# A gated cross-attention block on one core: SyncE's turn in another order, context for two pairs at once, and the sums read back from the scratch in one transfer

## The reference, cut to what matters

```
v, k = ctx @ Wv + bv, ctx @ Wk + bk          # per batch, 16 heads of 16
q    = layernorm(x) @ Wq + bq
energy = q . k, masked; attn = softmax(energy / 4)
x = x + tanh(g_xattn) * ((attn @ v) @ Wo + bo)
h = layernorm(x) @ W @ W1 @ W2
x = x + tanh(g_ffn) * tanh(h + bias)
```

## Time and profile before

| what | value |
|---|---|
| time, median of 3 runs (lowest, highest) | 1143.55 us (1141.15, 1146.37) |
| the profiled execution, its own time | 1153.29 us |
| its span in the profile | 1151.5 us |
| busy: PE / DVE / ACT / POOL | 90% / 81% / 72% / 70% |
| DMA engines, mean busy share in the steady part | 52% to 54% |
| granted TensorE clock, mean | 0.978 of full |

### The profile page before, as it was taken

The page is one execution under the profiler, slowest core; times in us unless marked ns, Lnnn a source line. Parts: engine busy times, 40 slices in busy tenths (PEclk is TensorE's granted clock), DMA queues, the critical chain, the costliest instruction groups (busy, mean ns, idle before and its releaser), DMA issues.

```text
span 1151.5 us, 45278 instructions
## 1 busy us (share of the span) xinstructions
PE 1041.1 (90%) x18487; PEld 905.1 (79%) x18487; DVE 937.6 (81%) x1331; ACT 834.5 (72%) x1275; POOL 801.2 (70%) x1184
## 2 busy tenths in 40 slices
PE   5989989999999999999999989989999999999964
PEld 4767878887888888888778778878788788888854
DVE  4778788788888888888888788788887787888766
ACT  4466778677787777777787777777776786777742
POOL 5256677677777777777777777677776676777753
PEclk9899999999999999999999999999998999999998
DMA  5134455555555555555555455555545454554432
GB/s 154 41 95 128 130 141 152 139 142 153 145 155 139 154 152 145 148 154 155 139 154 143 140 150 144 144 145 144 161 133 138 139 144 137 140 159 122 115 114 90
DMA packets 260400, 158.87 MB, mean 138 GB/s; under 512 B 174945, under 2 KB 227170, under 8 KB 260194
## 3 DMA queue, kind: packets, MB, share of 16 engines
q1 hardware_dynamic: 260050, 155.72, 48.5%
q10 hardware_dynamic: 144, 0.26, 0.1%
HBM read 85.92 MB, written 68.94 MB: 134 GB/s over the span
## 4 chain that ended last, share of the span: by engine, by line
PE 34%; DMA 26%; SPq 23%; issue 11%; DVE 5%; POOL 1%; ACT 0%; DVEq 0%; POOLq 0%
DMA scratch_y<-yn 12%; PE ps_m L502 8%; PE ps_s L623 6%; SPq L299 6%; PE ps_s L602 6%; DMA q_aug<-scratch_m 5%; SPq L288 4%; DMA scratch_m<-max_T 4%; PE ps_m L564 4%; PE ps_m L495 4%; SPq L271 3%; PE ps_x L634 2%; PE ps_s L608 2%; SPq L258 2%; SPq L281 2%
## 5 line engine op out<-in xcount | busy, mean ns | idle before, releaser
L1006 DVE TENSOR_TENSOR probs<-ps_s,far_T 128x2048 f32<-128x2048 f32 x128 | 293.3, 2291 | 99.5 <-PE ps_s L623 93.2
L995 DVE TENSOR_REDUCE neg_max<-ps_s 128x16 f32<-128x2048 f32 x128 | 292.6, 2286 | 60.0 <-PE ps_s L608 59.8
L797 ACT ACTIVATE probs<-probs 128x2048 f32<-128x2048 f32 x128 | 244.6, 1911 | 6.7 <-DVE probs L1006 6.6
L623 PE MATMUL ps_s<-q_aug,k_aug 32*128 32x128 f32 x4096 | 155.4, 289 | 62.7 <-DMA q_aug<-scratch_m 59.1
L623 PEld LDWEIGHTS ps_s<-q_aug,k_aug 32*128 32x128 f32 x4096 | 130.3, 191 | 83.4 <-DMA q_aug<-scratch_m 69.1
L413 POOL TENSOR_TENSOR cT<-ctx_T,cT 128x512 fp32r<-128x512 f32 x62 | 79.2, 1277 | 151.6 <-ACT cT L747 151.6
L772 ACT ACTIVATE q_aug<-ps_m,q_bias,q_scale 128x256 f32<-128x256 f32 x256 | 123.4, 562 | 70.9 <-PE ps_m L495 63.3
L602 PE MATMUL ps_s<-k_aug,q_aug 32*128 32x128 f32 x4096 | 151.9, 284 | 14.4 <-DVE probs L1006 7.4
L602 PEld LDWEIGHTS ps_s<-k_aug,q_aug 32*128 32x128 f32 x4096 | 129.3, 187 | 35.1 <-issue 27.4
L634 PE MATMUL ps_x<-probs,v_ones 128*32 128x128 f32 x4096 | 139.2, 277 | 3.2 <-issue 2.4
L772 ACT ACTIVATE k_aug<-ps_m,k_bias,parity 128x256 f32<-128x256 f32 x256 | 123.5, 564 | 18.1 <-PE ps_m L495 18.1
(11 more groups left out here) (123 smaller groups left out, 1789.5 us busy)
## 6 DMA issues: line engine op xcount, KB each, us to landing
scratch_a<-a_den SPq DMA_DIRECT2D x64, 512.0 KB, 3.4
x_in<-in_x SPq DMA_DIRECT2D x64, 256.0 KB, 3.9
a_rows<-scratch_a SPq DMA_DIRECT2D x64, 256.0 KB
den_wide<-scratch_r SPq DMA_DIRECT2D x64, 256.0 KB
out<-y SPq DMA_DIRECT2D x64, 256.0 KB, 4.9
ctx_in<-in_ctx SPq DMA_DIRECT2D x252, 64.0 KB, 3.4
scratch_y<-yn SPq DMA_DIRECT2D x59, 256.0 KB, 4.7
y_blocks<-scratch_y SPq DMA_DIRECT2D x236, 64.0 KB, 2.1
```

The costliest lines, as they stand in the source:

```text
L623: last = nc.tensor.matmul(ps_s[:, j, s, :], k_aug[p % 2][rows, n, s, :], q_aug[p % 2][rows, n, s, :], start=True, stop=True, tile_position ...
L797: nc.scalar.activation(tile, tile, ACT.Exp).then_inc(probs_ready, 1)
L995: nc.vector.tensor_reduce(neg_max[:, 0:H].rearrange("p (j c) -> p j c", j=G), ps_s[:], AX.X, ALU.max, negate=True).then_inc(max_ready, 1)
L1006: nc.vector.tensor_tensor(probs[i % 2][:].rearrange("p j s q -> p (j s) q"), ps_s[:].rearrange("p j s q -> p (j s) q"), far_T[:].unsqueeze ...
```

## The change

Four things:

1. On SyncE, `write_y(t-4)` moves from the end of the turn to a place ahead of `read_max(2t+1)` and `read_wide(t-2)`. `load_x` moves behind `read_max(2t)`.
2. `load_ctx` takes two pairs at once (four transfers of 128 KB in place of eight of 64 KB), in every second turn, and stands behind `read_max(2t)` and `load_x` instead of ahead of `read_y`. The first pair has a tile of its own.
3. `read_den` reads the sums in one transfer, from `scratch_a`, and so waits until `write_a` has landed; it moves behind `read_max(2t)`. ScalarE's `keep_a` no longer waits for it; `write_a` does.
4. On VectorE, `reciprocals(t-2)` moves behind `turn_max(2t+1)`, and `turn_ctx(t+2)` behind `turn_max(2t)` and `add_residual(t-4)`.

```diff
-            def load_ctx(p):
-                wait(sp, ctx_turned, p - 1)
...
+            def load_ctx(g):
+                pairs = 2 if is_pair(2 * g + 2) else 1
+                first = PAIR * (2 * g + 1)
+                wait(sp, ctx_turned, 2 * g - 1)
                 for a in range(G):
                     rows = slice(a * 32, (a + 1) * 32)
...
+                    sp.dma_start(ctx_in[g % 2][rows, 0:PAIR * pairs].rearrange("c n (b e) -> c (n b) e", e=64),
+                                 ctx[first:first + PAIR * pairs, :, a * 64:(a + 1) * 64].rearrange("n (b c) e -> c (n b) e", c=32)
+                                 ).then_inc(ctx_landed[g % 2], 16)
...
             def write_a(p):
                 sp.wait_ge(a_ready, 2 * p + 2)
                 wait(sp, a_landed, 16 * p)
+                wait(sp, den_landed, 16 * p)
...
             def read_den(p):
-
-                sp.wait_ge(a_ready, 2 * p + 2)
+                sp.wait_ge(sa_landed, 16 * (p + 1))
                 wait(sp, recip_ready, p)
-                for a in range(2):
-                    sp.dma_start(den[a * 64:(a + 1) * 64], a_den[p % 2][D::ROWS, a].rearrange("j m n q -> j (m n q)")).then_inc(den_landed, 16)
+                sums = scratch_a.rearrange("a (j r) c -> (a j) r c", j=G)[:, D, :]
+                sp.dma_start(den[:], sums).then_inc(den_landed, 16)
...
-                if is_pair(t + 3):
-                    load_ctx(t + 3)
                 if is_pair(t - 5):
                     read_y(t - 5)
                 write_max(2 * t)
                 if is_pair(t - 2):
+                    write_a(t - 2)
+                read_max(2 * t)
+                if is_pair(t - 2):
                     read_den(t - 2)
-                    write_a(t - 2)
                 if is_pair(t + 4):
                     load_x(t + 4)
-                read_max(2 * t)
+                if t % 2 == 0 and is_pair(t + 3):
+                    load_ctx((t + 2) // 2)
                 write_max(2 * t + 1)
                 if is_pair(t - 2):
                     write_reciprocals(t - 2)
                     read_a(t - 2)
+                if is_pair(t - 4) and t - 4 <= END:
+                    write_y(t - 4)
                 read_max(2 * t + 1)
                 if is_pair(t - 2):
                     read_wide(t - 2)
-                if is_pair(t - 4) and t - 4 <= END:
-                    write_y(t - 4)
...
-                if is_pair(t + 2):
-                    turn_ctx(t + 2)
                 turn_max(2 * t)
                 if is_pair(t - 4):
                     add_residual(t - 4)
+                if is_pair(t + 2):
+                    turn_ctx(t + 2)
...
+                turn_max(2 * t + 1)
                 if is_pair(t - 2):
                     reciprocals(t - 2)
-                turn_max(2 * t + 1)
```

More of the change, by code:

```diff
@@ L72, in gated_xattn_block @@
         x_in = [sb(f"x_in{i}", [P, PAIR, E]) for i in range(X_RING)]
-        ctx_in = [sb(f"ctx_in{i}", [P, PAIR, E]) for i in range(2)]
+        ctx_first = sb("ctx_first", [P, PAIR, E])
+        ctx_in = [sb(f"ctx_in{i}", [P, 2 * PAIR, E]) for i in range(2)]
         ctx_T = sb("ctx_T", [P, KT, TOK])
@@ L126, in gated_xattn_block @@
         x_landed = [sem(f"x_landed{i}") for i in range(X_RING)]
+        ctx_first_landed = sem("ctx_first_landed")
         ctx_landed = [sem(f"ctx_landed{i}") for i in range(2)]
@@ L176, in yn_of @@
         def yn_of(p):
-            return ctx_in[0] if p == NP - 1 else yn
+            return ctx_first if p == NP - 1 else yn
         def yT_of(p):
@@ L202, in load_x, with load_first_ctx @@
                 sp.dma_start(x_in[p % X_RING][:], x_v[:, p]).then_inc(x_landed[p % X_RING], 16)
-            def load_ctx(p):
-                wait(sp, ctx_turned, p - 1)
-                if p == 0:
-                    sp.dma_start(ctx_in[0][:], ctx_v[:, 0]).then_inc(ctx_landed[0], 16)
-                    return
+            def load_first_ctx():
+                sp.dma_start(ctx_first[:], ctx_v[:, 0]).then_inc(ctx_first_landed, 16)
+            def load_ctx(g):
+                pairs = 2 if is_pair(2 * g + 2) else 1
+                first = PAIR * (2 * g + 1)
+                wait(sp, ctx_turned, 2 * g - 1)
                 for a in range(G):
                     rows = slice(a * 32, (a + 1) * 32)
-                    sp.dma_start(ctx_in[p % 2][rows].rearrange("c n (b e) -> c (n b) e", e=64),
-                                 ctx[PAIR * p:PAIR * (p + 1), :, a * 64:(a + 1) * 64].rearrange("n (b c) e -> c (n b) e", c=32)
-                                 ).then_inc(ctx_landed[p % 2], 16)
+                    sp.dma_start(ctx_in[g % 2][rows, 0:PAIR * pairs].rearrange("c n (b e) -> c (n b) e", e=64),
+                                 ctx[first:first + PAIR * pairs, :, a * 64:(a + 1) * 64].rearrange("n (b c) e -> c (n b) e", c=32)
+                                 ).then_inc(ctx_landed[g % 2], 16)
             def load_first():
                 load_x(0)
-                load_ctx(0)
+                load_first_ctx()
                 load_weight(wq_raw, Wq, wq_landed)
@@ L226, in load_first @@
                     sp.dma_start(mask_4[r * ROWS:(r + 1) * ROWS], mask[0, 0].rearrange("(c i) k -> i c k", i=ROWS)).then_inc(mask_landed, 16)
-                load_ctx(1)
+                load_ctx(0)
                 load_x(2)
@@ L246, in load_later @@
                 sp.dma_start(bf_wide[:], b_ffn.rearrange("(a n) -> a n", a=1).to_broadcast([P, E])).then_inc(bf_landed, 16)
-                load_ctx(2)
                 load_x(3)
@@ L329, in _ @@
                     read_wide(t - 2)
-                if is_pair(t - 4) and t - 4 <= END:
-                    write_y(t - 4)
             y3, y2, y1, last = NP - 4, NP - 3, NP - 2, NP - 1
             store(NP - 7)
+            write_a(y1)
             read_den(y1)
-            write_a(y1)
             write_reciprocals(y1)
@@ L338, in _ @@
             read_wide(y1)
+            write_a(last)
             read_den(last)
-            write_a(last)
             store(NP - 6)
@@ L506, in turn_first_ctx @@
             def turn_first_ctx():
-                pe.wait_ge(ctx_landed[0], 16)
+                pe.wait_ge(ctx_first_landed, 16)
                 for k in range(KT):
@@ L510, in turn_first_ctx @@
                         last = nc.tensor.transpose(bank("cT", 0)[:, k * TOK + b * P:k * TOK + (b + 1) * P],
-                                                   ctx_in[0][:, b, k::KT], ident[:])
+                                                   ctx_first[:, b, k::KT], ident[:])
                 last.then_inc(ctx_turned, 1)
@@ L802, in keep_a @@
                 wait(act, sa_landed, 16 * (p - 1))
-                wait(act, den_landed, 32 * (p - 1))
                 nc.scalar.activation(a_den[p % 2][:, :, :, n, :].rearrange("p a m q -> p m a q"),
@@ L959, in turn_ctx @@
             def turn_ctx(p):
-                dve.wait_ge(ctx_landed[p % 2], 16 * G * (p // 2) + (16 if p % 2 == 0 else 16 * G))
+                g, i = (p - 1) // 2, (p - 1) % 2
+                dve.wait_ge(ctx_landed[g % 2], 16 * G * (g // 2 + 1))
                 wait(dve, cT_ready, p)
                 nc.vector.transpose(ctx_T[:].rearrange("p k (g c) -> p g k c", c=32),
-                                    ctx_in[p % 2][:].rearrange("p n (b r k) -> p (n b) k r", k=KT, r=32)).then_inc(ctx_turned, 1)
+                                    ctx_in[g % 2][:, i * PAIR:(i + 1) * PAIR].rearrange("p n (b r k) -> p (n b) k r", k=KT, r=32)).then_inc(ctx_turned, 1)
             def low_of_ctx(p):
@@ L1028, in reciprocals @@
             def reciprocals(p):
-                dve.wait_ge(den_landed, 32 * (p + 1))
+                dve.wait_ge(den_landed, 16 * (p + 1))
                 wait(dve, r_landed, 16 * p)
```

## The result

The changed kernel takes 1150.46 us (median of 14 runs, 1145.55 to 1154.48) against 1143.16 us for the kernel before on the same chip (14 runs): a ratio of 1.0093, 95% interval 1.0067 to 1.012. The profiled execution of the changed kernel took 1152.93 us, with a span of 1151.1 us, 0.4 us less than that of the kernel before. Its mean granted TensorE clock was 0.987, against 0.978, so the clock is not what the change lost.

The account below looks back on a forecast made before the run. The prediction took TensorE, held by SyncE's chain, to bound the kernel before, and a new 17.5 us loop through GpSimd and SyncE to bind afterwards. 27 + 6 - 2 + 3 = +34 us gave 1177 us, range 1120 to 1210.

Parts of the forecast that it names:

- The loop: GpSimd's `a_norm` to `yn`, then SyncE's `write_y`, `read_max`, `read_wide` to the next `a_norm`: 17.5 us a turn, +27 us.
- The place to which TensorE's wait went: TensorE's 1.25 us wait a turn was to move to ScalarE's `aT` and the `q_aug` spread behind it.
- `read_wide` to `a_norm`: From SyncE's issue of `read_wide` to GpSimd's start of `a_norm`: taken as 5.2 us, from rows of 4.18 to 5.35.
- the stretch: Time from `read_wide`'s issue to the start of `a_norm`; forecast 5.2 us.
- The quiet row of 4.85 us: `read_wide` to `a_norm` at the end of the kernel, with hardly another transfer; read as showing little gain from empty surroundings.
- The other terms, 10.56, 0.1, 0.46 and 1.19: In us: `a_norm` to end of `yn`; semaphore allowance; `write_y` to next issue; `read_max`'s issues to `read_wide`. Together 12.31.
- The sum of +34 us: Whole forecast change: GpSimd's turn +27, context +6, start -2, end +3 us, on the profiled 1153.3 us.
- The context's +6 us: SyncE's round in turns with context, 17.9 us beside 17.5, in 29 turns: +6 us, bounds 0 and +12.
- 2.67 us in the open: The context's issues on SyncE, formerly hidden in the wait for `scratch_y`, now stand uncovered in every second turn.
- I take 0: Sums waiting for `scratch_a` cost VectorE's `reciprocals` nothing while SyncE is under 1.5 us late; far end +29 us.
- The faster one: Rival: `read_wide` to `a_norm` takes 4.18 us, turn 16.5 us, time 1111 us; decides at 4.74 us; chance 0.16.
- The third, SyncE's round: Rival: 128 KB context issues take twice as long, SyncE's round 20.6 us, +90 us; includes VectorE stopped at `reciprocals`; chance 0.09.

Follow-up runs that it names:

- the first experiment: The changed kernel with `write_y` put back to the end of SyncE's turn, behind `read_wide`, all other edits kept: 1204.51 us, ratio 1.0422 to the kernel before.
- the third group: Runs on one chip: before 1151.07 us, changed 1149.50, changed with `read_max(2t+1)` behind `read_wide` 1124.50, the same with the sums as before 1115.15.

## Why the prediction was wrong, point by point

**The mechanism was right.** The loop from `a_norm` over `yn`, `write_y`, `read_max` and `read_wide` to the next `a_norm` closes in the changed kernel and sets its turn; the wait for `yn` in 58 turns, GpSimd's 42% of the chain, and the 25 us that went when `read_max` left the loop show it. The place to which TensorE's wait went was forecast in part. ScalarE's wait at `aT` rose from 30.0 to 100.6 us, as forecast, but TensorE's own new wait is for GpSimd's `xn`, 64.8 us in 57 places, which the forecast did not name.

**The term that was mis-sized: `read_wide` to `a_norm`.** I took 5.2 us, "since `write_y`'s 256 KB now go ahead of `den_wide`", and measured is 4.6. That alone is 36 us in 58 turns, of which the other terms below give back 11. The place of `write_y` costs the stretch nothing that the runs show: 4.58 us with it ahead of `den_wide` and 4.56 behind it, all other edits kept. The stretch fell to 4.67 us by moving `write_y` alone and to 4.74 by moving the context alone. Why it falls stays open. The quiet row of 4.85 us at the end was no lower bound either; there `read_wide` followed `read_a` by 0.7 us, in the changed kernel by 4.3 us at the median. That distance is not the reason by itself: in the first experiment it is 2.2 us and with `read_max` out of the loop 2.1 us, at stretches of 4.56 and 4.52 us, and 2.0 us in the kernel before, at 5.03. The other terms, 10.56, 0.1, 0.46 and 1.19, measured 10.8, 0.03, 0.43 and 1.22; the row of 10.56 was a short one, the median of before is 10.8 too. Together 17.1 us in place of 17.5: 0.43 us a turn, 25 us in 58 turns, out of the 33 forecast. The sum of +34 us was made on the profiled execution, and between the two profiled executions the difference is -0.4 us: -0.5 in the 58 turns, where I had +27 for the loop and +6 for the context, -6.1 at the start, where I had -2, and +6.2 at the end, where I had +3.

**The base of the sum.** I added the difference to the median of the runs but took the turn of 17.05 us from a profiled execution that was 10 us above it. The changed kernel's profiled execution lies 2.5 us above its median. So the profiles give a steady part that is equal, and the clocked runs a difference of 7.3 us. This worked the other way and hid part of the error above. The result also depends on the chip: the changed kernel had 1150.46 and 1149.50 us on two occasions, the kernel before between 1143 and 1158, and the ratio was 1.0093 once and 1.0007 once. That a loop through a fixed piece of GpSimd's work varies less than a chain through transfers fits these numbers; it was not tested by itself.

**The context's +6 us** did not appear: the loop binds in turns with and without context alike, 17.0 us both. In front of `write_y` SyncE stood 1.9 us in turns with context and 2.2 us in the others (medians), so its round was about 15.1 and 14.8 us, where I had 17.9 and 15.2. That four issues of 128 KB cost no more than four of 64 KB was right: 2.20 us in the timeline of the first experiment against 2.67. But "2.67 us in the open" was right as a mechanism: it is what makes the turns alternate once `write_y` is late or `read_wide` is ahead of it. What I did not count is that `scratch_y` lands in 2.8 us in place of 4.7: from `write_y` to `read_y` it is 3.0 us in place of 4.8 (medians), and I had put 5.03 for it in SyncE's round. Over two turns that saves 3.7 us, more than the 2.6 us of the context's four issues.

**The sums.** "I take 0" held for VectorE, which waited only 3 times in the changed kernel, because SyncE was early enough. Without the early `write_y`, in the first experiment, it waited 50 times, 61.4 us in all. And "0" was wrong in all: with the old sums the kernel reads 0.9888 of before, and in the third group, at equal order, 0.992 of the other (1115.15 / 1124.50), about 9 us. Part of it is the end: from the last `write_y` on it takes 65.0 to 70.3 us in the seven profiles with the sums from the scratch, and 60.0 to 64.5 in the seven with the old sums. I had +3 us for it. The start gained 3 to 6 us (first `write_y` at 96.6 and 98.5 us, against 102.7 and 101.8), where I had 2. By the start's rows x for pair 3 came 1.6 us sooner to VectorE; the rest was not traced.

**The rivals.** The faster one asked for a stretch under 4.74 us, from the base of 17.05. The stretch went under it, to 4.6, and still the kernel was not faster: GpSimd's part is 10.8 and not 10.56 us in most turns, and the base was too high. The third, SyncE's round, did not bind in the changed kernel, which had 1.9 us of room in it; but three of the experiments (`write_y` back, the context alone, `read_wide` first) ran into it at once. By the Trainium skill's fit ("DMA: Bandwidth & Descriptors", section "Anatomy of one DMA — SWDGE (gpsimd) path") 256 KB issued from GpSimd would take 2.6 us, which is an estimate from that page. No run here issued `den_wide` from GpSimd, and issued from SyncE no stretch was under 3.6 us.

## What to carry to other kernels

Before moving a step ahead in an engine's list, write down for every step that it passes who waits for it a turn later; if the moved step waits for that same engine, the list closes a loop, and its length is a sum of rows. Then ask which of the passed steps need be in it: here two issues moved by one place gave 2.2%. And when a wait is filled with issues of other work, moving that work away exposes the wait; whether the whole is a gain depends on how soon the transfer lands in its new place, which is to be measured and not taken from its old place.

## What the hardware showed that I had not expected

The landing of one transfer of 256 KB depended on how long nothing had been issued ahead of it. The page's median for `scratch_y` is 4.7 us in the kernel before and 2.8 us in the changed kernel:

```profile
scratch_y<-yn SPq DMA_DIRECT2D x59, 256.0 KB, 4.7
```

```profile
scratch_y<-yn SPq DMA_DIRECT2D x59, 256.0 KB, 2.8
```

At first sight the order decides, since it is 4.4 to 4.9 us in the six profiles in which `write_y` follows `den_wide`, and 2.7 to 3.4 us in the eight in which it goes ahead of it. But in those eight SyncE also stands still in front of `write_y`, for `yn`, 0.8 to 2.2 us at the median. Sorted by that pause, over all 14 profiles:

| `write_y` follows | pause ahead of it | times | median landing |
|---|---|---|---|
| `read_wide` | at most 0.42 us | 354 | 4.7 us |
| `read_a` | under 0.5 us | 40 | 4.4 us |
| `read_a` | 0.5 to 1.5 us | 208 | 3.3 us |
| `read_a` | over 1.5 us | 224 | 2.7 us |

Two turns of the version with the new order alone (`read_wide` behind `write_y`, context and sums as before) show it side by side:

```profile
1043.20 0.60 SPq L277 DMA_DIRECT2D a_rows<-scratch_a  x1
1046.15 0.36 SPq L293 DMA_DIRECT2D scratch_y<-yn  x1
...
1060.42 0.60 SPq L277 DMA_DIRECT2D a_rows<-scratch_a  x1
1061.11 0.41 SPq L293 DMA_DIRECT2D scratch_y<-yn  x1
```

The first `scratch_y` landed 2.54 us after its issue, the second 4.42 us. So most of the fall goes with the pause that the loop itself brings, and little with the order. Whether it is the `a_rows` transfer still under way that holds `scratch_y` back, or something else that goes with the pause, no run here separates.

GpSimd's small steps are not of one length either. The same `ln_t` step over 128x4 elements (L380) took from 0.20 to 0.80 us in the changed kernel, with a median of 0.51, and 0.80 us in the turn shown. And of the 58 turns of the changed kernel 33 last 17.08 us and 9 last 16.79 us, each within 0.05 us. No run here says why.
